# Moving three pieces of work inside the step of a hand-ordered local-attention pipeline

## The reference

```
for i in range(DEPTH):                      # 6 layers
    x = attn_layer(shift_tokens(x), Wqkv[i], q_scale[i], k_scale[i], Wo[i]) + x
    x = ffn_layer(shift_tokens(x), ...) + x
# attn_layer, 16 heads of 64, windows of 32 tokens
q, k, v = split(x @ Wqkv)
q, k = l2norm(q) * qs, l2norm(k) * ksc
q = q * cos * scale + rotate_half(q) * sin * scale      # k: 1 / scale
sim = einsum(q, keys of this window and the one before) * 8, masked
out = softmax(sim) @ v ;  return out @ Wo
```

## Time and profile before

| what | value |
|---|---|
| median of three executions | 2109.46 us |
| time of the profiled execution | 2108.28 us |
| its span, first to last instruction | 2106.5 us |
| PE busy | 1912.5 us (91%) |
| DVE busy | 1685.5 us (80%) |
| ACT busy | 1447.3 us (69%) |
| POOL busy | 1249.9 us (59%) |
| ordinary step of stage B | 3.21 us |

### The profile page before, as it was taken

How to read it: one execution, slowest core, us unless ns; L and a number is a source line. 1 busy time by engine, 2 the same in 40 slices (tenths; PEclk the granted TensorE clock), 3 DMA queues, 4 the chain that set the end, 5 groups by cost and what they waited for, 6 DMA issues and landing times. The chain is left out here.

```text
span 2106.5 us, 79458 instructions
## 1 busy us (share of the span) xinstructions
PE 1912.5 (91%) x33524; PEld 1425.7 (68%) x33524; DVE 1685.5 (80%) x3905; ACT 1447.3 (69%) x5112; POOL 1249.9 (59%) x871
## 2 busy tenths in 40 slices
PE   5769999999999999999999999999999995493496
PEld 2358778687686886868868778687786872252374
DVE  5679889698796996978969889698796965696654
ACT  4269779598695995968959789597795972342121
POOL 2259778398694895957959669587593851031000
PEclk8879999999999999999999999999999998696798
DMA  3011112021120211212112121021120110001000
GB/s 115 0 44 43 32 51 57 22 78 37 41 61 22 77 42 35 58 31 72 42 29 61 41 56 53 20 69 46 41 58 19 41 33 13 0 2 62 1 1 21
DMA packets 88230, 85.72 MB, mean 41 GB/s; under 512 B 15393, under 2 KB 83009, under 8 KB 87233
## 3 DMA queue, kind: packets, MB, share of 16 engines
q1 hardware_dynamic: 87872, 80.63, 13.9%
HBM read 25.51 MB, written 1.05 MB: 13 GB/s over the span
## 5 line engine op out<-in xcount | busy, mean ns | idle before, releaser
L1082 POOL TENSOR_TENSOR RN<-N,minus_half 128x8 f32<-128x8 f32 x384 | 633.0, 1648 | 287.6 <-DVE N L1010 287.6
L920 ACT ACTIVATE PB<-PS,NMX 128x64 f32<-128x64 f32 x1536 | 462.4, 314 | 30.9 <-DVE NMX L1036 30.6
L679 PE MATMUL PS<-WQ,XS 128*128 128x256 f32 x1536 | 398.8, 383 | 7.1 <-SPq L623 6.2
L920 ACT ACTIVATION_READ_ACCUMULATOR PB<-PS,NMX 128x1 f32 x1536 | 313.2, 204 | 0.0
L679 PEld LDWEIGHTS PS<-WQ,XS 128*128 128x128 f32 x1536 | 264.7, 192 | 28.7 <-SPq L623 6.6
L886 ACT ACTIVATE SQ<-PS 128x512 f32<-128x512 f32 x384 | 229.6, 598 | 49.3 <-PE PS L679 11.4
L1010 DVE TENSOR_REDUCE N<-SQ 128x8 f32<-128x512 f32 x384 | 259.6, 676 | 0.0
L1024 DVE SCALAR_TENSOR_TENSOR QK<-RN,RR 128x512 f32<-128x512 f32 x384 | 254.3, 662 | 1.0 <-POOL RR L1077 1.0
L763 PE MATMUL PS<-ident,QK 128*128 128x128 f32 x1536 | 251.9, 287 | 1.2 <-DVE QK L1024 1.2
L1077 POOL TENSOR_TENSOR RR<-R1B,R2B 128x512 f32<-128x512 f32 x192 | 244.8, 1275 | 0.2 <-DVE QK L1024 0.2
L1077 POOL TENSOR_TENSOR RR<-R 128x512 f32<-128x512 f32 x192 | 244.8, 1275 | 0.0
(11 more groups left out here) (270 smaller groups left out, 3519.6 us busy)
## 6 DMA issues: line engine op xcount, KB each, us to landing
VS<-XB SPq DMA_DIRECT2D x384, 96.0 KB, 2.2
VS<-XB SPq DMA_DIRECT2D x288, 32.0 KB, 2.0
WQ<-in_wqkv SPq DMA_DIRECT2D x40, 192.0 KB, 2.7
WO<-in_wo SPq DMA_DIRECT2D x6, 512.0 KB, 3.9
XS<-XT SPq DMA_DIRECT2D x10, 256.0 KB, 3.3
XS<-XT SPq DMA_DIRECT2D x10, 255.8 KB, 4.0
BIG<-in_wgu SPq DMA_DIRECT2D x1, 2048.0 KB, 8.0
W<-in_w SPq DMA_DIRECT2D x6, 341.0 KB, 3.2
```

The source lines that it names most:

```text
L679: mm = nc.tensor.matmul(PQ[:, m % 2, j * 256:(j + 1) * 256], XSb[b][:, t0:t0 + P], WQ[:, pair * 384:pair * 384 + 256], start=True, stop=True)
L920: ex = nc.scalar.activation(PB[:, g % 2, u, :], SC[:, h, DH * t:DH * t + DH], ACT.Exp, bias=NMX[:, u:u + 1], accum_out=PSUMS[:, g % 2, u:u ...
L1082: nc.gpsimd.tensor_tensor(RN[:, g % 2, :], N2[:, g % 2, :], minus_half[:, :], ALU.pow)
```

## The change

Three pieces of work are put elsewhere in their engine's step; no instruction is added or removed, and units and buffers stay as they are.

- PE: `project_qk(g + 3)` goes from behind the value matmuls to the very start of the step, ahead of the transposes of `QK`.
- ACT: `squares(g + 3)` goes behind the copy to `XB`.
- DVE: the reciprocal goes ahead of the sine product, and the product that makes `QK` goes from between reciprocal and normalisation to behind the maxima.

The new orders are, PE: 679, 763, 776, 784, 798, 810, 826; ACT: 903, 892, 913, 886, 920; DVE: 1009, 1010, 1021, 1014, 1030, 1036, 1024. In a tail step the product for `QK` still stands ahead of the feed-forward block.

```diff
 def step(g):                                   # PE
+    if there(g + 3) and not tail:
+        project_qk(g + 3)
     if there(g):
         pe.wait_ge(qk_in.sem, qk_in.take())
...
         last.then_inc(vp_ps.sem, 1)
-    if there(g + 3) and not tail:
-        project_qk(g + 3)
     if tail:
         down(1)
...
     if there(g - 4) and not feed_forward_at(g - 1):   # ACT
         outputs(g - 4)
-    if there(g + 3) and not feed_forward_at(g - 1):
-        squares(g + 3)
     if values or probs:
...
+    if there(g + 3) and not feed_forward_at(g - 1):
+        squares(g + 3)
     if there(g):
         act.wait_ge(nmx_in.sem, nmx_in.take())
...
     k = (g - 1) % 2                            # DVE
+    if there(g - 1):
+        dve.wait_ge(sc_free.sem, g)
+        nc.vector.reciprocal(RO[:, k, :], PSUMS[:, k, :]).then_inc(ro_in.sem, 1)
     if there(g + 2):
         nc.vector.tensor_tensor(R2s[g % 2] ...).then_inc(rot_in.sem, 1)
-    if there(g - 1):
-        dve.wait_ge(sc_free.sem, g)
-        nc.vector.reciprocal(RO[:, k, :], PSUMS[:, k, :]).then_inc(ro_in.sem, 1)
-    if there(g + 1):
-        dve.wait_ge(rr_in.sem, rr_in.take())
-        nc.vector.scalar_tensor_tensor(QKg[(g + 1) % 2], ...).then_inc(qk_in.sem, 1)
     if there(g - 1):
         dve.wait_ge(ro_in.sem, ro_in.take())
...
     if there(g) and not tail:
         maxima()
+    if there(g + 1):
+        dve.wait_ge(rr_in.sem, rr_in.take())
+        nc.vector.scalar_tensor_tensor(QKg[(g + 1) % 2], ...).then_inc(qk_in.sem, 1)
     if tail:
         feed_forward(*tail)
```

More of the change, by code:

```diff
@@ L1043, in step @@
                             maxima()
+                        if there(g + 1):
+                            dve.wait_ge(rr_in.sem, rr_in.take())
+                            nc.vector.scalar_tensor_tensor(QKg[(g + 1) % 2], RN[:, (g + 1) % 2, :].unsqueeze(2)
+                                                           .to_broadcast([P, 8, DH]), 1e12, RRg,
+                                                           ALU.min, ALU.mult)\
+                                .then_inc(qk_in.sem, 1)
                         if tail:
```

## The result

| | before | after |
|---|---|---|
| median of the executions, us | 2108.95 (4) | 2125.56 (4) |
| range, us | 2108.28 to 2109.92 | 2125.30 to 2126.13 |
| span of the profiled execution, us | 2106.5 | 2123.6 |

The ratio is 1.0079 with a 95% interval of 1.0061 to 1.0096: the change makes the kernel 16.6 us slower. Forecast were 2128 us and a range of 2118 to 2142.

What follows compares the result with a forecast made beforehand. PE was taken to bound the kernel at 3.21 us a step; 366 steps x 0.05 us of bare load added 18.3 us, all else 0, so 2109.5 + 18.3 = 2128 us, 0.9% slower, range 2118 to 2142.

Steps and rivals of the forecast that it cites:

- PE sets the step: Ordinary step before the change: PE's own instructions fill 3.21 us without idle time, while DVE needs 3.11 us.
- The bare load, +0.05 us: First weight load behind line 826, uncovered: a transpose's 0.057 to 0.06 goes, that of XS, 0.105 to 0.11, comes.
- rival B: Load behind line 826: equally long for both kinds or hidden by the tile switch, so no change, 2109 us; chance 0.08.
- 366 steps: Steps paying the bare load: 377 with line 826 ahead and a projection, less 11 tail steps; 18.3 us in all.
- Transposes to scores, T + 1.30: From the first transpose at T, PE and ACT's copy to QKT both allow the scores at T + 1.30; cost 0.
- Rival A: ACT's copy to QKT comes to set the step, 0.02 to 0.08 late, 2135 to 2157 us; chance 0.14.
- T + 2.42: Earliest start of ACT's exponentials after the first transpose at T, about 0.07 to 0.1 behind the maxima; nothing on the path.
- Rival C: PE's pause behind line 826 is really a wait for QK; step falls to DVE's 3.11, 2073 us; chance 0.06.
- DVE and ACT costed at nothing: The new ACT and DVE orders add no time: exponentials have 0.3 us left, DVE needs 3.11 us in 3.26.
- 0.1 us of slack for `QK`: DVE in the changed order: QK ends at T + 2.97, PE's pulled-ahead load comes some 0.2 before T + 3.26.
- `QK` could be later by 0.7 for nothing: Old order: QK is done 0.74 us before its transposes start, so its product can move later by 0.7 us free.
- let it wait only behind tails: DVE's reciprocal ahead of the sine product waits for exponentials only behind a tail, some 0.3 us, absorbed by DVE's slack.

Runs made afterwards that it cites:

- pe_alone: The kernel before with only the PE edit (projection first in the step), ACT and DVE as before: 2125.23 us, ratio 1.0076.
- bf16_probabilities: The kernel before with the probabilities PB held in bf16 and turned by bf16 matmuls: 2090.12 us, ratio 0.9903.
- squares_alone: The kernel before with the ACT edit alone (squares behind the copy to XB): 2109.31 us, ratio 0.9996.
- transposes_first_qk_early: The changed kernel with the DVE order of before and the projection behind the transposes of QK, ahead of probabilities and values: 2110.75 us, ratio 1.0003.
- values_first_qk_early: The changed kernel with the DVE order of before, value matmuls first in the step and the projection back where it was: 2124.26 us, ratio 1.0070.
- extra_transpose: The changed kernel with one more 128 x 128 transpose of old data ahead of the projection: 2148.41 us, ratio 1.0181.
- probabilities_first: The changed kernel with the DVE order of before; PE order transposes of PB, projection, transposes of QK, values, mask, scores: 2183.42 us, ratio 1.0347.
- act_dve_alone: The kernel before with the ACT and DVE edits alone, PE order as before: 2351.63 us, ratio 1.1150.

## Why the prediction was right, step by step

- PE sets the step: right. A change on PE alone gives the whole result (`pe_alone`), one that only relieves PE gives a gain (`bf16_probabilities`), and at this step neither the place of the squares nor an earlier projection matters (`squares_alone`, `transposes_first_qk_early`).
- The bare load, +0.05 us: right in kind, a little too large. Measured were 3.256 - 3.211 = 0.045, and the first projection matmul took 0.48 (forecast 0.49, under rival B 0.44). It goes with the neighbour of line 826, whichever work it is (`values_first_qk_early`), and not with the projection's place (`transposes_first_qk_early`).
- 366 steps: 366 x 0.045 = 16.5 us, against 16.6 in the medians and 2123.6 - 2106.5 = 17.1 in the spans. The start was put at +-1 us; from the first to the tenth cosine product the changed kernel gains 0.8 us. Inside the feed-forward blocks nothing moved: such a step and the one behind it take 38.82 us together against 38.77, the 0.05 of the one ordinary start among them. At the last residual of stage B (line 977) the profiles lie 1779.50 - 1763.19 = 16.3 us apart; the other 0.8 of the spans comes behind stage B, where nothing was changed. No new wait showed at the projection's semaphores.
- Transposes to scores, T + 1.30: right, 1.28 when measured tight. Rival A was the near miss. The exponentials start at T + 2.35 (508.40 - 506.05), not at T + 2.42; nothing hung on it.
- Rival B, no change by the page's rule on load time: fell. The Trainium skill, page "TensorE: Matmul & The Clock Gate", section "LDWEIGHTS (loading the stationary operand)", has the columns alone count. The traces disagree, and they decide: float32 loads of 128 columns cost 0.10 us (`XS`) and 0.057 us (transposes) when nothing covers them.
- Rival C, a hidden wait for `QK`: fell. Nothing in any run got below 3.21 as long as PE's work was the same.
- DVE and ACT costed at nothing: right for the three edits together, and this is the part that the experiments, not the prediction, priced. The prediction found 0.1 us of slack for `QK` in the changed order, and that is there: `QK` ends at 505.02 + 0.68 = 505.70, and PE loads it at 505.83. POOL's sum now waits for `QK` in every step, some 0.4 us, and keeps up as was assumed. But it said that `QK` could be later by 0.7 for nothing also in the old one. That was read off a single distance, without following the loop over the maxima: made last on DVE, with PE's old order, `QK` comes too late by 0.68 a step. Likewise the reciprocal: the prediction let it wait only behind tails, which holds with the `QK` product behind the maxima and not otherwise (+0.17 a step). No sum of the prediction rested on either, so the forecast came out right, but its word that the old order leaves `QK` 0.7 us was wrong.

## What to carry to other kernels

When an engine has no idle time, order still has a price: look at which instruction follows a switch of the array's tile size, since its weight load is not covered there, and give the place to the kind with the shortest load. A reordering is priced by loops, not by the slack at one point: add up each way around (scores, maxima, `QK`, transposes) for the new order before calling a move free. A loop can close over two steps, as that over the squares does, and it shows only when the step gets shorter. And a piece of an edit can be harmful alone and free beside another (the DVE edit without the PE edit costs 0.68 us a step), so a half that fares badly alone is no proof against the whole.

## What the runs showed that was not expected

- Some ACT and DVE instructions changed their length with no edit to themselves, as the groups by line of the profile after show (count, busy us, mean ns, idle before):

```profile
L920 ACT ACTIVATE PB<-PS,NMX 128x64 f32<-128x64 f32 x1536 | 471.4, 337 | 29.9 <-DVE NMX L1030 29.8
L1040 DVE SCALAR_TENSOR_TENSOR QK<-RN,RR 128x512 f32<-128x512 f32 x384 | 261.8, 682 | 0.6 <-POOL RR L1077 0.6
```

  The exponentials took 314 ns before and 337 after, `QK` 662 and 682, the sine product 681 and 661. The other traces show what each goes with. The exponentials take 330 to 337 ns in the four kernels whose projection stands ahead of the transposes of `QK` (the changed one, `pe_alone` 336, `extra_transpose`, `probabilities_first`), and 311 to 314 in the ten others, `act_dve_alone` among them. On DVE the long product right behind the reciprocal takes 660 to 663 ns and the other of the two 681 or 682, in all fourteen: the change only swaps them. Why is open, and it stayed off the path here.
- An uncovered or half covered load can appear between two matmuls of the same tile size too, when the matmul before it is short (0.055 us in bf16, where the load of `XS` needs 0.11).
